# A two-layer graph network in one program: the first layer's front in another order, with wider steps

## What is computed

```python
h = maximum(layernorm(x), 0)                     # layer 0
e = leaky(h[src] @ attn_w[:32] + h[dst] @ attn_w[32:])
alpha = segment_softmax(e, dst)
x = x + segment_sum(h[src] * alpha, dst)
h = maximum(layernorm(x), 0)                     # layer 1
msg = einsum over 16 bases of w_comp[etype], weight, h[src]
a = maximum(tanh(relu(((h[src] @ A1.T + b1) * (h[dst] @ A2.T + b2 + rel_emb[etype])).sum() / sqrt(32))), 0)
x = x + relu(segment_sum(a * msg, dst) + h[src[last edge of node]] @ self_loop_weight)
```

## Time and profile before

| | us |
|---|---|
| median of 3 runs | 10141.72 |
| lowest, highest run | 10138.01, 10142.83 |
| the profiled execution's own time | 10141.45 |
| its span | 10140.1 |
| POOL busy in the span | 7445.1 |
| DVE, ACT, PE busy in the span | 2061.1, 1168.4, 474.4 |

### The profile page before, as it was taken

How to read it: one execution, slowest core, us unless ns; L and a number is a source line. 1 busy time by engine, 2 the same in 40 slices (tenths; PEclk the granted TensorE clock), 3 DMA queues, 4 the chain that set the end, 5 groups by cost and what they waited for, 6 DMA issues and landing times.

```text
span 10140.1 us, 21586 instructions
## 1 busy us (share of the span) xinstructions
PE 474.4 (5%) x2054; PEld 225.3 (2%) x2054; DVE 2061.1 (20%) x2223; ACT 1168.4 (12%) x1579; POOL 7445.1 (73%) x7050
## 2 busy tenths in 40 slices
PE   0000000000000000000463000000000000000000
PEld 0000000000000000000121000000000000000000
DVE  5411111111111100111332222222222222222222
ACT  0010000000000000000353101111111111100110
POOL 6677777777777777777445777777777777777776
PEclk9999999999999999999887555555555555555555
DMA  3321111111111111111697222222222222222221
GB/s 85 104 54 39 38 38 38 38 38 38 38 38 38 31 36 38 38 38 38 238 389 273 63 61 61 61 61 61 61 61 61 61 61 57 61 57 61 61 61 33
DMA packets 315210, 711.76 MB, mean 70 GB/s; under 512 B 150288, under 2 KB 209117, under 8 KB 294446
## 3 DMA queue, kind: packets, MB, share of 16 engines
q0 software_dynamic: 230048, 250.74, 14.2%
q1 hardware_dynamic: 84989, 459.15, 11.8%
q10 hardware_dynamic: 144, 1.61, 0.0%
HBM read 316.82 MB, written 393.07 MB: 70 GB/s over the span
## 4 chain that ended last, share of the span: by engine, by line
POOL 66%; issue 26%; DMA 3%; DVE 3%; another core or an unknown queue 1%; PE 1%; ACT 1%; SPq 0%; POOLq 0%; ACTq 0%; DVEq 0%
POOL arena L553 64%; DMA layer_rows<-arena 3%; DVE ps L930 1%; POOL dst_score_at_starts L586 1%; POOL aggregate_nodes L553 1%; PE ps L822 0%; PE ps L821 0%; DVE dst_score_of_edge L953 0%; DVE arena L1071 0%; ACT arena L671 0%; ACT arena L706 0%; DVE arena L1012 0%; DVE arena L1090 0%; DMA attention_weights<-in_L_gnn_attn_w 0%
## 5 line engine op out<-in xcount | busy, mean ns | idle before, releaser
L553 POOL DMA_INDIRECT arena<-layer_rows,edge_row_index x6448 | 6853.7, 1063 | 2153.4 <-issue 2102.7
L1000 DVE TENSOR_TENSOR arena<-arena,ps 128x62 f32<-128x62 f32 x52 | 13.9, 268 | 3421.6 <-DMA arena<-layer_rows,edge_row_index 3421.6
L1120 DVE TENSOR_TENSOR h_nodes<-arena,ps 128x124 f32<-128x124 f32 x52 | 19.4, 373 | 2991.6 <-DMA arena<-layer_rows,edge_row_index 2991.6
L662 ACT ACTIVATE ps<-arena 128x62 f32<-128x62 f32 x52 | 11.8, 226 | 3551.9 <-issue 3547.7
L743 ACT ACTIVATE ps<-arena 128x62 f32<-128x62 f32 x52 | 11.8, 226 | 3470.3 <-issue 2048.1
L1114 DVE TENSOR_TENSOR_SCAN ps<-arena,ps 128x2016 f32<-128x2016 f32 x52 | 226.8, 4362 | 401.6 <-issue 271.4
L621 POOL DMA_INDIRECT y_hat_at_starts<-aggregate_nodes,start_index x98 | 100.4, 1024 | 251.2 <-ACT arena L706 121.1
L821 PE MATMUL ps<-weights_a,arena 128*128 128x512 bf16 x588 | 249.1, 424 | 117.5 <-ACT arena L706 78.4
L822 PE MATMUL ps<-weights_b,arena 128*128 128x512 bf16 x588 | 241.3, 423 | 0.0
L842 PE MATMUL ps<-identity,arena 128*32 128x128 f32 x104 | 31.6, 408 | 4407.8 <-issue 4066.9
L553 POOL DMA_INDIRECT aggregate_nodes<-layer_scans,last_edge_index x196 | 191.8, 978 | 62.7 <-issue 57.1
(11 more groups left out here) (195 smaller groups left out, 2205.0 us busy)
## 6 DMA issues: line engine op xcount, KB each, us to landing
layer_rows<-arena SPq DMA_DIRECT2D x98, 2107.0 KB
arena<-layer_rows,edge_row_index POOLq DMA_INDIRECT x6448
layer_scans<-arena SPq DMA_DIRECT2D x52, 1085.0 KB
y_hat_at_starts<-zeros SPq DMA_DIRECT2D x52, 992.0 KB
arena<-y_hat_at_starts SPq DMA_DIRECT2D x52, 992.0 KB
layer_scans<-arena SPq DMA_DIRECT2D x52, 992.0 KB
even_odd_relation<-arena SPq DMA_DIRECT2D x1, 3224.0 KB
even_odd<-even_odd_relation SPq DMA_DIRECT2D x52, 62.0 KB
```

The costliest lines, as they stand in the source:

```text
L553: pool.indirect_dma_start(tile, None, table, bass.IndirectOffsetOnAxis(ap=index, axis=0)) \
```

## The change

What it does, part by part:

1. **Loads.** SP's loads of `x` go out after a smaller memset, and the edges are issued only when `x` and the attention weights have landed; `src` is now first of the three, and the store of padded `src` waits for `src` alone (`s_src_in`).
2. **Norm in halves.** The layer norm of layer 0 runs over 49 nodes twice, interleaved; ACT squares and takes roots by halves.
3. **Counts for seven nodes at once.** The 7 instructions L953 of a half of `blocks` become one comparison of 3584 elements into `le` and one sum (`le` is new space in `arena`, 7168 to 10752). The half is reported free after the comparison.
4. **Bounds by a shifted copy.** `start` of 97 nodes is a copy of `end` in SBUF; only the partition's last end goes through DRAM (128 values of 4 bytes each way). The scatter indices of the 97 are ready first, the one of node 0 later.
5. **Group 3's gathers in waits.** Ten are issued before the wait for `kblk`, six between the block gathers and the scatters, 46 after. The start score and the scatter of node 0 go to the end of the scatters.

```diff
@@ sync
+            sp.wait_ge(s_set, 2)
+            sp.wait_ge(s_x, 5 * 16)
-            for tile, ap in ((dsti, dst), (srci, src), (eti, etype)):
+            for tile, ap, landed in ((srci, src, s_src_in), (dsti, dst, s_in), (eti, etype, s_in)):
...
-            sp.wait_ge(s_in, 12 * 16)
+            sp.wait_ge(s_src_in, 4 * 16)
             src_c = src_d.rearrange("(p t) c -> p (t c)", t=T)
             sp.dma_start(src_c, srci).then_inc(s_src_d, 16)
...
             sp.wait_ge(s_end, 1)
-            sp.dma_start(end_d[1:1 + NP].rearrange("(p j) -> p j", j=J), end[:, :]).then_inc(s_end_d, 16)
+            sp.dma_start(end_d[1:1 + P].rearrange("(p j) -> p j", j=1), end[:, J - 1:J],
+                         allow_slow_non_contiguous=True).then_inc(s_end_d, 16)
             sp.wait_ge(s_end_d, 32)
-            sp.dma_start(start[:, :], end_d[0:NP].rearrange("(p j) -> p j", j=J)).then_inc(s_start, 16)
+            sp.dma_start(start[:, 0:1], end_d[0:P].rearrange("(p j) -> p j", j=1),
+                         allow_slow_non_contiguous=True).then_inc(s_start, 16)
@@ gpsimd
+        INDEX, START = 10, 6
             first0(2)
+            first0(3, 0, INDEX)
             pool.wait_ge(s_kblk, 1)
...
-            pool.wait_ge(s_nodeidx, 1)
+            first0(3, INDEX, INDEX + START)
             pool.wait_ge(s_zero_d, 64)
             pool.wait_ge(s_sdst_d, 16)
-            gather(y0init, sdst_d, first_u[:, 0:1], s_y0init)
-            for j in range(J):
-                pool.indirect_dma_start(z0_d, ...
-            first0(3)
+            pool.wait_ge(s_nodeidx, 1)
+            for j in range(1, J):
+                score_at_start(j)
+            gather(y0init, sdst_d, first_u[:, 0:1], s_y0init)
+            pool.wait_ge(s_nodeidx, 2)
+            score_at_start(0)
+            first0(3, INDEX + START, K)
@@ vector
-            v.memset(xt[:, :, :], 0.0)
+            v.memset(xt[:, n_rest:J, :], 0.0).then_inc(s_set, 1)
...
+            for at in halves:
+                done(v.tensor_reduce(small[:, at], xt[:, at, :], AX.X, ALU.add))
+                done(v.tensor_scalar(small[:, at], small[:, at], -1.0 / D, None, ALU.mult))
+                v.tensor_tensor(h0[:, at, :], xt[:, at, :], spread(small[:, at], [P, J // 2, D]), ALU.add) \
+                    .then_inc(s_centered, 1)
...
             for q in range(J // SH):
                 v.wait_ge(s_blk[q % 2], 16 * SH * (q // 2 + 1))
-                for i in range(SH):
-                    j = q * SH + i
-                    ins = v.tensor_scalar(junk[:, 0:EB], blocks[:, j % SB, :], nidp[:, j:j + 1], None, ALU.is_le,
-                                          ALU.add, accum_out=ccnt[:, j:j + 1])
-                    if i < SH - 1:
-                        done(ins)
-                ins.then_inc(s_blk_used, 1)
+                at, half = slice(q * SH, (q + 1) * SH), q % 2 * SH
+                v.tensor_tensor(le, blocks[:, half:half + SH, :], spread(nidp[:, at], [P, SH, EB]), ALU.is_le) \
+                    .then_inc(s_blk_used, 1)
                 v.wait_ge(s_blk_used, q + 1)
+                done(v.tensor_reduce(ccnt[:, at], le, AX.X, ALU.add))
...
+            done(v.tensor_copy(start[:, 1:J], end[:, 0:J - 1]))
+            starts(slice(1, J))
             v.wait_ge(s_start, 16)
-            done(v.tensor_tensor(nonempty[:, :], start[:, :], end[:, :], ALU.is_lt))
...
+            done(v.tensor_scalar(last[:, :], end[:, :], -1.0, 0.0, ALU.add, ALU.max))
+            starts(slice(0, 1))
```

More of the change, by code:

```diff
@@ L246, in build @@
         s_in = sem("s_in")
+        s_src_in = sem("s_src_in")
         s_x = sem("s_x")
@@ L268, in build @@
         s_sq = sem("s_sq")
+        s_centered = sem("s_centered")
+        s_var = sem("s_var")
+        s_std = sem("s_std")
         s_sdst = sem("s_sdst")
@@ L348, in build @@
         FIRST = SEG * (CHUNKS - 2) + TB
+        halves = [slice(0, J // 2), slice(J // 2, J)]
         whole = P - 1
@@ L563, in _, with first0 @@
             pool.wait_ge(s_feat0_d, 16)
-            def first0(b):
+            def first0(b, lo=0, hi=K):
                 pool.wait_ge(s_idx0[b], 16)
-                for k in range(K):
+                for k in range(lo, hi):
                     gather(g0[b][:, k, :], feat0_d, idx[:, b, k:k + 1], s_g0[b])
@@ L639, in _ @@
         def _(act):
-            act.wait_ge(s_sqrt_in, 1)
-            act.activation(curr[:, 0:J, :], feat0[:, :, 0:D], ACT.Square).then_inc(s_sq, 1)
-            act.wait_ge(s_sqrt_in, 2)
-            act.activation(rstd[:, :], small[:, :], ACT.Sqrt).then_inc(s_sqrt, 1)
+            for i, at in enumerate(halves):
+                act.wait_ge(s_centered, i + 1)
+                act.activation(curr[:, at, :], feat0[:, at, 0:D], ACT.Square).then_inc(s_sq, 1)
+            for i, at in enumerate(halves):
+                act.wait_ge(s_var, i + 1)
+                act.activation(rstd[:, at], small[:, at], ACT.Sqrt).then_inc(s_std, 1)
             act.wait_ge(s_pool_init, 4)
@@ L877, in _, with layer_norm @@
             roots = [0]
-            def layer_norm(at, count, xc, sq, to, square=None):
+            def layer_norm(at, count, xc, sq, to):
                 sm, wide = small[:, at], [P, count, D]
```

42 lines of the change are left out of this document (25 added, 17 removed).

## The result

| | before | after |
|---|---|---|
| median of the runs, us | 10139.12 (22 runs, 10135.47 to 10142.83) | 10123.39 (22 runs, 10120.75 to 10126.41) |
| ratio, 95% interval | | 0.9985 (0.9978 to 0.9991) |
| span of the profiled execution | 10140.1 | 10121.6 |
| first gather / first block gather | 52.42 / 303.54 | 50.97 / 311.27 |
| first transfer of the scores | 468.51 | 450.68 |

15.7 us faster where 44 were forecast, and outside the range. It is 0.16%, less than the forecast said that a measurement of this kernel can tell from no change, though the two sets of runs don't overlap. The two profiled executions are 18.2 us apart (10141.45 and 10123.23): that of the kernel before lies 2.3 above its median, so the traces show some 2.5 us more than the medians.

A forecast was written before the change was run, and what follows sets the result against it. POOL's list of indirect DMAs, one every 1.25 us, was taken as the bound, so reaching group 4 earlier was the gain: -4.3 + 27.5 + 1.0 + 20.0 = 44.2 us off 10141.5, giving 10097.3; range 10085 to 10114.

The forecast's parts named there:

- First gather: POOL's first gather of node rows: starts at 51.0, was 52.42; the third gather starts at 55.8.
- Block indices: POOL's wait for `kblk`: first block gather moves from 303.54 to 307.8, 4.3 us lost.
- Count for seven: Block gathers: no waits left for DVE's counts, 124.1 us in place of 151.6, gain 27.5.
- Bounds: From last block gather to the scatters: 12.4 us against 13.36, gain 1.0.
- Group 3: Gathers after the scatters: 46 left instead of 62, 20.0 us gained.
- Rival 1: DVE's counts before `kblk`: slow stretch does not move with instruction count, `kblk` 1.4 earlier; 10091.6, chance 0.20.
- Rivals 2 and 3: 2: new DVE instructions slow gathers beside them, 10110 to 10122, chance 0.14; 3: SBUF passes hold POOL, 10208, chance 0.04.
- Rival 4: Block gathers: POOL still waits for halves of `blocks`; 10100 to 10114, chance 0.06.

The follow-up runs named there:

- dve_14_memsets: Changed kernel with fourteen one-element memsets on DVE ahead of the 98 counts; 10122.00 us where the kernel before takes near 10139.
- no_gathers_moved_2: Changed kernel with group 3's sixteen gathers back behind the scatters; 10122.02 us where the kernel before takes near 10139.
- count_one_by_one_3: Changed kernel with the comparison of gathered blocks node by node again; 10128.60 us where the kernel before takes near 10139.
- pool_64_memsets_2: Changed kernel with 64 one-element memsets on POOL ahead of the loop over groups; median 15.7 us below the kernel before, which takes near 10139.

## Why the prediction was wrong

The step that failed is the first one: "Groups follow each other at that pace to the end of layer 0, and nothing behind the front changes. What the change is worth is therefore how much earlier POOL reaches group 4." It was read from the earlier trace rows, all of the front, where POOL had its margin. The two slow gathers of the loops stood in a stretch whose mean is 1.40, and I took them for the exceptions. The windows of the same trace, 144 gathers in 200 us, would have shown a steady pace that no row of the front has. By the lead rule the front's time before the scores counts on a limited chip only up to the last wait that fills POOL's margin; before, that wait stood ahead of the scores (13.36 us), the change shortened it to 4.45 behind six gathers, and of 35.3 us POOL gave back 17. The forecast's 44.2 and the measured 15.7 are apart by 28.5: 8.9 are terms of the front that came out smaller, 17.0 the lead given back, and 2.6 the difference between traces and medians.

The terms, one by one:

- **First gather** at 51.0: 50.97. The gather at 55.8 that was to be the third is the second, 55.49; the third starts 4.1 earlier than before, not 5.0.
- **Block indices** 4.3 later: 7.7. The 24 to 25 fast counts are right (the first full gap of 1.68 is ahead of the 25th, at 99.64), but the samples are only 0.1 earlier, not 1.4, the 98 counts take 7.2 longer, not 5.7 (the last starts at 304.04), and from it to the first block gather are 0.7 more.
- **Count for seven**, 27.5: 25.1. Comparison and sum take 3.89 each (4.02 and 3.91 forecast), and POOL waits for neither:

```profile
332.48 3.89 DVE L982 TENSOR_TENSOR arena<-arena,ps 128x3584 f32<-128x3584 f32 x1 [0.92 <-DMA arena<-dst_float,block_index]
336.40 3.89 DVE L985 TENSOR_REDUCE count_in_block<-arena 128x7 f32<-128x3584 f32 x1
```

  The first block gather costs 1.2 and not 1.9 more than the others, but ten starts from the 75th gather on are 1.30 to 2.09 apart and cost 3.2, where POOL is some 24 us ahead of one transfer per 1.40: the margin seems to run out here for the first time. In dve_14_memsets, where POOL comes 9.8 us later to the blocks, there are none of them. The term is the largest of the sum and right in mechanism on this chip; on an unlimited one it is 0, since its cause, DVE's slow instructions, isn't there.
- **Bounds**, 1.0: 0.5. **Group 3**, 20.0: 18.4 at its place, nothing that could be seen at the end, and 0.5 at group 9 (no_gathers_moved_2).
- **Rival 1** fell: the slow stretch moved with the instruction count, and again with 14 memsets. **Rivals 2 and 3** fell: of the 73 block gathers behind the first, beside L982 and L985, each takes 0.94 to 0.95. Some of the last 24 take 0.99 to 1.24 and one 1.78 (at 431.04), but in dve_14_memsets, with the same instructions on DVE, all 97 behind the first take 0.94 to 0.96, so it is not DVE that stretches them. The Trainium skill, "SBUF — State Buffer", section "Who interferes with whom", says that a DVE instruction with at most one SBUF input outside the two-port modes does not contend with GpSimd, and L982 and L985 agree with it. With two SBUF inputs, it says, DVE contends with a GpSimd instruction that reads SBUF; the gathers of 4 us beside L957 and L958, which have two, fit that. It infers that `tensor_tensor` leaves the writing of descriptors alone; the gather of 3.85 us beside L971, a `tensor_tensor`, says otherwise, and the measurement decides. **Rival 4** fell, no wait.
- "Instruction fetch mechanics" of the Trainium skill's "Runtime: NRT & Kernel Launch" says fetching is mostly hidden: the unlimited chips agree (98 counts 1.16 apart), the limited ones show 2.80 from about the 84th instruction on. Whether that is fetching no run here shows. The forecast weighed this page against its rows and kept the rows, rightly for its chip.

None of the rivals was the one that came true: that POOL's own pace in the loops takes back a lead.

**What stays open.** What the limit is. It touches POOL (1.40 a gather, memsets too), DVE (0.75 us of delay for a memset, 2.80 a count with its accumulator read) and PE (2.80 for a matmul with its weight load), each after a stock of instructions and with bursts between, on some chips and not on others. My guess is that it lies in how instructions or their records reach or leave the engines, but no run here separates these, and no run was made without the profiler's records. The lead rule is fitted: with its points chosen as above it is right to some 3 us at group 9 in the nine traces of limited chips, and the largest miss is that of the memsets (679.4 - 623 = 56.4, so 5.4 by the rule, where 2.3 were measured). With all points taken behind the long gathers the kernel before is 6 us off. What the traces show without the rule: on limited chips a delay of 23.1 us at group 4 (count_one_by_one_3) leaves 3.7 at group 9, one of 27.9 (pool_64_memsets_2) leaves 2.3, and on an unlimited one a lead of 10.2 is kept to the end.

## What to carry to other kernels

Before you price a lead, compare the engine's mean spacing over a long steady stretch (instructions in a window) with its spacing in the place you change: if the mean is longer, some supply is the bound, and a lead is kept only as far as the engine had been idle long enough. Two edits that each remove the same wait don't add, and leaving out each in turn shows it. And a gain that hangs on an odd spacing (1.68 us of nothing before a 1.06 us instruction) may belong to the chip and not to the kernel: look for it on another before building on it.

## What the runs showed of the hardware

- The same program takes 10139 or 9205 us from one chip to another (two of the five against three): 934 us for 7042 indirect transfers, whose spacing in the loops is 1.40 or 1.25 us in the mean.
- On the limited chips POOL may be some 25 us ahead of that mean; 28 us of delay before the loop left 2.3 us at group 9, and none by the medians.
- DVE passes over 128 x 3224 words in SBUF stretch a gather beside them from 0.94 us to 3.5 to 4.4; a comparison of SBUF with PSUM and a sum of SBUF of 128 x 3584 leave it at 0.95, and so does a pass of 128 x 3224 with an accumulated sum (0.94). Loads that keep the DMA engines busy for 0.86 of the time leave it at 0.94.
